# Side jobs of VectorE and GpSimd dealt anew over the slots of a fused attention and FP4 feed-forward kernel

## The chip, the cores and the metric

One NeuronCore of a Trainium2 chip runs the whole kernel in one launch. The metric is the time of one execution on the device in microseconds (us), the median of several runs. Differences of up to about 0.3% can't be told from none.

## The reference

For 16 sequences of 512 tokens with 128 features: a layer norm, then x + attention(xn) + ffn(xn).

```python
q  = (xn @ Wqa @ Wqb)              # 16 heads of 8
k, v = (xn @ Wkva @ Wkvb)          # 4 heads of 8, each shared by 4 query heads
q, k = rope(q), rope(k)
w  = softmax(causal(q @ k.T * 8**-0.5))
attention = (w @ v) @ Wout + bout

def fp4(x):                        # blocks of 16 along the last dimension
    scale = max(max|x| / 6, 1e-12)
    return nearest_of(0, .5, 1, 1.5, 2, 3, 4, 6)(|x / scale|) * sign(x) * scale
ffn = fp4(silu(fp4(xn) @ fp4(w_gate).T) * (fp4(xn) @ fp4(w_up).T)) @ fp4(w_down).T    # 352 hidden
```

## The kernel before

The kernel is one software pipeline over the batches (sequences). Each engine runs its own program of iterations T = -3 to 16, and in iteration T it works on several batches at once: batch T+3's statistics and norm, batch T+2's projections and rope, batch T+1's score maxima and the hidden layer's gate and up products, batch T's exponentials, weighted sums and FP4 rounding of h, and batch T-1's output. A job for a batch outside 0 to 15 is left out, so the first iterations hold little. Semaphores alone order the engines; within an engine the order is that of the program.

An iteration has 8 slots, one for each pair of heads. In a slot TensorE computes six tiles of scores for the row maxima (written (slot, tile) below; three PSUM buffers max_ps in turn, each read by one VectorE reduction of 512, 384 or 256 columns), five tiles of scores for the exponentials (two buffers exp_ps, read by ScalarE), the misc jobs of that slot (two buffers misc_ps: 0 and 1), and a half of one group's weighted sums. Tile n of the maxima waits until VectorE has read tile n-3. The misc jobs are given by a table: gate0 and up0 and then the transposes of xn in slot 0; q and then gate1 and up1 in slot 1; mrow1, qrot and kk in slot 2; gate2, up2 and v in slot 3; gate3 and up3 in slot 4; xqT and out0 in slot 5; out1 and mrow0 in slot 6; the three transposes of h (hqT0 to hqT2, L1152) in slot 7. Output rows are onT times Wout plus three chunks (128, 128, 96 rows) of the FFN's last product (L1164, L1166).

Between the reductions (L713) VectorE does its side jobs, each after a given tile:

- slot 0: `scales` for h (L662 to L666: three small steps to h_scale and h_inv), gated(0) (L726), `magnitudes` of x (L673 and L675 on x_mag)
- slot 1: q_cos (L799), hidden_max(0) (L735), gated(1); slot 2: q_sin (L809), hidden_max(1), k_cos and k_sin
- slot 3: invert(T-1, 1) (L744), the four bn_stats (L831) and bn_aggr (L839), gated(2), the copy of v to v_stage
- slot 4: `magnitudes` of h (L673, L675 on h_mag, 1408 columns of bf16) between (4,0) and (4,1), gated(3), hidden_max(2)
- slot 5: the product onT (L755, two inputs in SBUF), hidden_max(3), output(0); slot 6: maximum of x, output(1); slot 7: `scales` for x, invert(T, 0).

GpSimd, in its order: the causal selects of group 3 (L529, four instructions), split_rest (L552, needs ScalarE's split_high, L962), hidden(0) (L561, h = gate_sb * up_half, 352 columns), steps 1 to 3 of x's rounding (L539, L542, L545; step 1 needs both magnitudes), step 0 of h's (L536, h * h_inv, 1408 columns, needs the h scales), hidden(1), the selects of group 0, V from v_stage (L605), the adds and splits of q and k, hidden(2), the selects of group 1, the variance to rstd (L569 to L574; L572 is a power of 128x4 elements), hidden(3), steps 1 and 2 of h (L539 "h+mag", L542), the selects of group 2, step 3 of h (L545), x_bias = x_res + bias (L643), step 0 of x (L650). TensorE's transposes of h wait for L545; hidden(f) waits for gated(f).

ScalarE evicts and exponentiates; in slot 0, after tile 0, it does split_high and the copy to x_mag (L1010), and after tile 1 th and up_half (L932, L945) of gate0 and up0.

SyncE issues all DMAs. At the start it loads constants, waits until all have landed, and only then runs its iterations; in each, the load of x_in for batch T+4 follows the output stores, and scatter_inverses(T, 0), which waits for invert(T, 0), stands ahead of the second half of the loads of K and Q.

## Time and profile before

| what | value |
|---|---|
| runs | 814.58 us median of 3 (814.21 to 816.49) |
| profiled execution | span 812.0 us from its first to its last instruction; the page gives no other time of it, so the 2.6 us up to the median lie around the span |
| TensorE matmul busy | 731.3 us, 90% |
| VectorE, ScalarE, GpSimd busy | 637.4, 545.0, 613.8 us |
| TensorE's granted clock | mean 0.977 of full; 1.00 in every stretch from 91 to 762 us |
| DMA | 76 MB, about a third of the DMA engines' time |

Every time below is in us from the span's start. A busy TensorE is one with a matmul in flight, so small gaps between starts don't show as idle. The steady part runs from 82 to about 754 us: one iteration every 44.8 us. In the timelines below the iteration of interest has its slots 3 to 7 between 232 and 260.5, and the next iteration's slot 0 begins at 260.5.

### The profile page before, as it was taken

The page shows a single profiled execution, that of the slowest core. Times are in us where ns is not written, and L with a number is a line of the kernel's source. Part 1 is how long each engine was busy: PE and PEld are TensorE (multiplying, and loading weights), DVE is VectorE, ACT ScalarE, POOL GpSimd, SP SyncE. Part 2 cuts the span into 40 slices and gives each one's busy share as a digit, 9 for nine tenths or more (in the row PEclk, how much of TensorE's full clock was granted, in tenths as well). Part 3 has the DMA queues.
Part 4 walks back from the last instruction along what each step waited for, and adds up shares of the span by engine and source line. Part 5 has one row for each costly group of instructions (what it writes and reads, how often), then busy time and mean ns, then how long its engine had stood idle before and what let it go on. Part 6 is the DMA issues. An engine that isn't in the chain of part 4 may idle for free.

```text
span 812.0 us, 18601 instructions
## 1 busy us (share of the span) xinstructions
PE 731.3 (90%) x6541; PEld 445.5 (55%) x6541; DVE 637.4 (78%) x1378; ACT 545.0 (67%) x1154; POOL 613.8 (76%) x707
## 2 busy tenths in 40 slices
PE   2366989999999999999999999999999999999782
PEld 1233545666656565656656565656566565656242
DVE  5569888989888888889898888888898888788200
ACT  1212777768777777777787777677777777575850
POOL 5533697878788897978787887979787888748470
PEclk9978899999999999999999999999999999999996
DMA  4423233333343334343333433343333433330211
GB/s 112 121 57 102 56 100 97 94 101 100 98 116 93 92 113 101 118 105 90 96 108 99 117 95 84 114 104 113 90 94 102 113 90 100 93 93 29 57 48 41
DMA packets 84438, 76.06 MB, mean 94 GB/s; under 512 B 27282, under 2 KB 66162, under 8 KB 84346
## 3 DMA queue, kind: packets, MB, share of 16 engines
q1 hardware_dynamic: 84346, 74.87, 33.9%
q8 instruction: 53, 0.87, 0.5%
q14 instruction: 39, 0.32, 0.1%
HBM read 40.73 MB, written 27.53 MB: 84 GB/s over the span
## 4 chain that ended last, share of the span: by engine, by line
PE 65%; DVE 8%; ACT 7%; DMA 6%; POOL 5%; issue 4%; SPq 4%; POOLq 0%; ACTq 0%; DVEq 0%
PE pv_ps L1109 16%; PE exp_ps L1088 12%; PE max_ps L1073 9%; PE misc_ps L1125 7%; PE max_ps L1074 5%; PE misc_ps L1166 5%; DVE neg_max L713 4%; PE misc_ps L1133 3%; ACT P L909 3%; DMA o_sum<-o_scr 2%; PE misc_ps L1164 2%; PE misc_ps L1152 2%; SPq L418 2%; PE misc_ps L1142 2%; DMA o_scr<-oT 1%
## 5 line engine op out<-in xcount | busy, mean ns | idle before, releaser
L713 DVE TENSOR_REDUCE neg_max<-max_ps 128x1 f32<-128x512 f32 (+3 forms) x768 | 430.6, 591 | 82.8 <-PE max_ps L1074 80.4
L909 ACT ACTIVATE P<-exp_ps 128x512 f32<-128x512 f32 x512 | 295.0, 599 | 166.4 <-PE exp_ps L1088 166.1
L1088 PE MATMUL exp_ps<-Q,K 128*128 128x512 bf16 (+3 forms) x1024 | 243.6, 301 | 9.0 <-ACT P L909 6.7
L1073 PE MATMUL max_ps<-K,Q 128*128 128x384 bf16 (+2 forms) x768 | 199.4, 278 | 24.6 <-DVE neg_max L713 13.5
L1074 PE MATMUL max_ps<-Kd,Q 128*128 128x128 bf16 x1024 | 190.9, 221 | 1.8 <-DVE neg_max L713 1.6
L529 POOL TENSOR_SCALAR_AFFINE_SELECT P<-P 128x512 f32<-128x512 f32 x256 | 162.8, 673 | 27.1 <-ACT P L912 27.1
L1109 PE MATMUL pv_ps<-P,V 128*32 128x512 f32 (+3 forms) x2048 | 164.2, 438 | 1.0 <-POOL P L529 0.8
L1073 PEld LDWEIGHTS max_ps<-K,Q 128*128 128x128 bf16 x768 | 75.1, 100 | 103.0 <-DVE neg_max L713 53.1
L1074 PEld LDWEIGHTS max_ps<-Kd,Q 128*128 128x128 bf16 x1024 | 97.9, 99 | 45.7 <-issue 23.0
L561 POOL TENSOR_TENSOR h<-gate_sb,up_half 128x352 f32<-128x352 f32 x64 | 59.8, 935 | 64.4 <-DVE gate_sb L726 64.4
L1088 PEld LDWEIGHTS exp_ps<-Q,K 128*128 128x128 bf16 x1024 | 81.8, 98 | 42.1 <-ACT P L909 20.5
L1109 PEld LDWEIGHTS pv_ps<-P,V 128*32 128x32 f32 x2048 | 53.6, 109 | 79.6 <-issue 68.5
L1125 PE MATMUL misc_ps<-wguT,xqT 128*128 128x352 f32 x256 | 90.1, 475 | 0.2 <-DVE q_cos L799 0.2
L912 ACT ACTIVATE P<-exp_ps 128x512 f32<-128x512 f32 x128 | 78.0, 610 | 15.5 <-PE exp_ps L1088 15.5
L1125 PEld LDWEIGHTS misc_ps<-wguT,xqT 128*128 128x128 f32 x256 | 48.1, 195 | 17.6 <-issue 1.2
L1166 PE MATMUL misc_ps<-wdT,hqT 128*128 128x128 f32 (+1 forms) x384 | 54.6, 279 | 0.0
L539 POOL TENSOR_TENSOR h<-h,h_mag 128x1408 f32<-128x1408 f32 x16 | 51.2, 3200 | 0.0
L1166 PEld LDWEIGHTS misc_ps<-wdT,hqT 128*128 128x128 f32 (+1 forms) x384 | 49.3, 196 | 0.0
L542 POOL TENSOR_TENSOR h<-h,h_mag 128x1408 f32<-128x1408 f32 x16 | 46.8, 2928 | 1.3
L744 DVE RECIPROCAL o_inv<-o_sum 128x32 f32<-128x32 f32 x32 | 11.3, 352 | 45.9 <-DMA o_sum<-o_scr 45.8
L536 POOL TENSOR_TENSOR h<-h,h_inv 128x1408 f32<-128x1408 f32 x16 | 41.5, 2592 | 0.3 <-DVE h_inv L666 0.3
L545 POOL TENSOR_TENSOR h<-h,h_scale 128x1408 f32<-128x1408 f32 x16 | 41.5, 2594 | 0.0
(108 smaller groups left out, 989.7 us busy)
## 6 DMA issues: line engine op xcount, KB each, us to landing
Q<-q_scr SPq DMA_DIRECT2D x64, 224.0 KB
o_scr<-oT SPq DMA_DIRECT2D x32, 256.0 KB, 3.5
q_scr<-q_split SPq DMA_DIRECT2D x16, 384.0 KB, 2.6
Kd<-K SPq DMA_DIRECT2D x64, 96.0 KB
x_in<-x SPq DMA_DIRECT2D x16, 256.0 KB, 4.6
q_scr<-q_split SPq DMA_DIRECT2D x16, 256.0 KB, 2.9
x_res<-x SPq DMA_DIRECT2D x16, 256.0 KB, 5.7
o_raw<-o_scr SPq DMA_DIRECT2D x32, 128.0 KB
```

The source lines that it names most:

```text
L529: nc.gpsimd.affine_select(out=diag, in_=diag, compare_op=ALU.is_ge, fill=0.0, base=0, pattern=[[0, GH], [1, 128]], channel_multiplier=-1). ...
L539: nc.gpsimd.tensor_tensor(t, t, mag[:, :], ALU.add).then_inc(quant, 1)
L561: nc.gpsimd.tensor_tensor(h[T.par(1)][:, f * F:(f + 1) * F], gate_sb[f % 2][:, :], up_half[f % 2][:, :], ALU.mult).then_inc(h_made, 1)
L713: nc.vector.tensor_reduce(neg_max[:, pr // 4, i, heads[0]:heads[0] + len(heads), pr % 4], max_ps[r % 3][:, 0:len(heads) * n].rearrange("p ...
L909: nc.scalar.activation(P[g % 2][:, hh + r % 2, col:col + 512], ps[:, :], ACT.Exp, scale=SCALE).then_inc(exp_done, 1)
L912: nc.scalar.activation(P[g % 2][:, hh:hh + 2, P_COL[2]:P_COL[2] + 256], ps[:, :].rearrange("p (h q) -> p h q", h=2), ACT.Exp, scale=SCALE) ...
L1073: nc.tensor.matmul(ps[:, col:col + d], Qt, Kt[:, half, g, 0:d], start=True, stop=True)
L1074: last = nc.tensor.matmul(ps[:, col + d:col + n], Qt, Kd[:, half, g, d:n], start=True, stop=True)
L1088: last = nc.tensor.matmul(exp_ps[n % 2][:, col:col + width], K[par][:, half, pr // 2, kb * 128:(kb + 1) * 128], Q[par][:, pr, kb * 128:S], ...
L1109: last = nc.tensor.matmul(pv_ps[32 * j:32 * j + 32, kb * 128:S], V[T.par(off)][:, kb, g, :], P[g % 2][:, j, P_COL[kb]:P_COL[kb] + width], ...
L1125: last = nc.tensor.matmul(ps[:, 0:F], xqT[T.par(1)][:, tok[f]], wguT[:, int(job[0] == "u"), :], start=True, stop=True)
L1166: last = nc.tensor.matmul(ps[:, tok[n]], hqT[0:cn, k, tok[c]], wdT[0:cn, k, :], start=False, stop=(k == 2))
```

## The change

- VectorE: `scales` for h of the next iteration's batch T+1 now stands in slot 7 between (7,3) and (7,4), no longer in slot 0; `magnitudes` of x comes after (0,5) instead of before it; the bn_stats are split, two after (1,5) and two after (2,5); the two steps of h's magnitudes are parted, the first after (4,0), the second after (4,4); hidden_max(3) goes from slot 5 to after (6,4); invert(T, 0) to the end of slot 7.
- GpSimd: step 0 of h (L536) is moved ahead of hidden(0) and of x's steps 1 to 3; x_bias and the copies to V are gone.
- ScalarE: split_high goes from after tile 0 to after tile 1 (behind th and up_half), x_mag from tile 0 to tile 2 of slot 0.
- V is written by VectorE in two copies straight from PSUM, into three tiles in turn; v_stage is gone.
- The bias is row 96 of the last chunk of wdT, met by a row of ones in hqT; output adds x_res alone. x_res is loaded one iteration later, at the head of SyncE's iteration.

```diff
+def third(self, off):
+return (self.t0 + off) % 3
...
 k_split = sb("k_split", [128, 3, 128], BF16)
-v_stage = sb("v_stage", [128, NT, KVH * D])
...
 Kd = sb("Kd", [128, 2, KVH, S], BF16)
-V = [sb(f"V{i}", [128, NT, KVH, 32]) for i in range(2)]
+V = [sb(f"V{i}", [128, NT, KVH, 32]) for i in range(3)]
 P = [sb(f"P{i}", [128, GH, P_WIDTH]) for i in range(2)]
...
     for dst, src in (
-        (bout_sb[:, :], bout.partition_broadcast(128)),
+        (wdT[FC[2][1]:FC[2][1] + 1, 2, :], bout.unsqueeze(0)),
         (w_raw[:, 768:768 + F], wdown),
...
     def iteration(T):
-        if T.has(0):
-            T.wait(sp, x_bias_done, 1, 0, 0)
-            sp.dma_start(x_res[:, :, :], x[T.batch(0)].rearrange("(c p) e -> p c e", p=128)).then_inc(x_res_loaded, 16)
+        if T.has(-1):
+            T.prev().misc_wait(sp, misc_read, "out1")
+            sp.dma_start(x_res[:, :, :], x[T.batch(-1)].rearrange("(c p) e -> p c e", p=128)).then_inc(x_res_loaded, 16)
         scatter_sums(T, -1, 1)
...
     nc.gpsimd.memset(half_neg[:, :], -0.5).then_inc(consts_set, 1)
-    for i in range(2):
+    for i in range(3):
         nc.gpsimd.memset(V[i][:, :, :, :], 0.0).then_inc(pool_const, 1)
...
     nc.gpsimd.memset(ident16[:, :], 0.0).then_inc(pool_const, 1)
-    pool.wait_ge(pool_const, 4)
-    for i in range(2):
+    pool.wait_ge(pool_const, 5)
+    for i in range(3):
...
         split_rest(T, 0, 1)
+        if T.has(0):
+            quantize(T, 0, 0, *hs)
         hidden(T, 0)
...
             nc.gpsimd.tensor_tensor(blocks(w_raw[:, :]), blocks(w_raw[:, :]), spread(w_inv[:, :]), ALU.mult).then_inc(w_step, 1)
-        if T.has(0):
-            quantize(T, 0, 0, *hs)
         hidden(T, 1)
...
             causal(T, 0, 0)
-        if T.has(1):
-            T.prev().misc_wait(pool, misc_read, "v")
-            if T.has(-1):
-                T.wait(pool, pv_done, KVH, -1, KVH)
-            for s in range(2):
-                nc.gpsimd.tensor_copy(V[T.par(1)][:, :, s::2, D * s:D * s + D],
-                                      v_stage[:, :, :].rearrange("p c (g d) -> p c g d", g=KVH)[:, :, s::2, :]).then_inc(v_ready, 1)
         if T.has(2):
...
             quantize(T, 0, 3, *hs)
-        if T.has(0):
-            T.wait(pool, x_res_loaded, 16, 0, 16)
-            T.misc_wait(pool, misc_read, "out1")
-            nc.gpsimd.tensor_tensor(x_bias[:, :, :], x_res[:, :, :],
-                                    bout_sb[:, :].unsqueeze(1).to_broadcast([128, NT, E]), ALU.add).then_inc(x_bias_done, 1)
         if T.has(3):
...
+    def powers_of_two(mag, sem_):
+        m = mag.bitcast(U16)
+        nc.vector.tensor_scalar(m, m, 0x7F80, 0x0040, ALU.bitwise_and, ALU.bitwise_or).then_inc(sem_, 1)
+    def at_least_one(mag, sem_):
+        nc.vector.tensor_scalar(mag, mag, 1.5 * 2.0 ** 22, None, ALU.max).then_inc(sem_, 1)
...
-        m = mag.bitcast(U16)
-        nc.vector.tensor_scalar(m, m, 0x7F80, 0x0040, ALU.bitwise_and, ALU.bitwise_or).then_inc(sem_, 1)
+        powers_of_two(mag, sem_)
         eng_wait(sem_, 1)
-        nc.vector.tensor_scalar(mag, mag, 1.5 * 2.0 ** 22, None, ALU.max).then_inc(sem_, 1)
+        at_least_one(mag, sem_)
...
         if n == 0:
-            T.wait(dve, x_bias_done, 1, -1, 1)
+            T.wait(dve, x_res_loaded, 16, -1, 16)
...
         nc.vector.tensor_tensor(y[:, c, :], misc_ps[0][:, 0:2 * E].rearrange("p (c e) -> p c e", c=2),
-                                x_bias[:, c, :], ALU.add).then_inc(misc_read[0], 1)
+                                x_res[:, c, :], ALU.add).then_inc(misc_read[0], 1)
+    def statistics(T, chunks):
+        if not T.has(3):
+            return
+        T.wait(dve, x_loaded, 16, 3, 16)
+        if 0 in chunks:
+            T.wait(dve, mv_done, NT, 2, NT)
+        for c in chunks:
+            nc.vector.bn_stats(bn_raw[:, c, :], x_in[:, c, :]).then_inc(bn_done, 1)
...
         reduces(0, 0, 1)
-        if T.has(0):
-            T.wait(dve, h_quant, 3, -1, 3)
-            T.wait(dve, h_maxed, NT, 0, NT)
-            scales(lambda s, n: T.wait(dve, s, 3, 0, n) if n else None, h_max[:, :], h_scale[:, :], h_inv[:, :], h_scales, 0)
         reduces(0, 2, 3)
         gated(T, 0)
-        reduces(0, 4)
+        reduces(0, 4, 5)
         if T.has(2):
...
             magnitudes(lambda s, n: T.wait(dve, s, 2, 2, n), x_mag[:, :], x_mags)
-        reduces(0, 5)
         first = T.t0 == FIRST_T + 1
...
         reduces(1, 5)
+        statistics(T, (0, 1))
...
         reduces(2, 5)
+        statistics(T, (2, 3))
...
         invert(T, -1, 1)
-        if T.has(3):
-            T.wait(dve, x_loaded, 16, 3, 16)
-            T.wait(dve, var_done, 2, 2, 2)
-            for c in range(NT):
-                nc.vector.bn_stats(bn_raw[:, c, :], x_in[:, c, :]).then_inc(bn_done, 1)
         reduces(3, 2)
...
+            T.wait(dve, var_done, 2, 2, 2)
             for c in range(NT):
...
-            T.wait(dve, v_ready, 2, 1, 2)
-            nc.vector.tensor_copy(v_stage[:, :, :], misc_ps[1][:, 0:128].rearrange("p (c n) -> p c n", c=NT)).then_inc(misc_read[1], 1)
+            if T.has(-1):
+                T.wait(dve, pv_done, KVH, -1, KVH)
+            for odd in range(2):
+                nc.vector.tensor_copy(V[T.third(2)][:, :, odd::2, D * odd:D * odd + D],
+                                      misc_ps[1][:, 0:128].rearrange("p (c g d) -> p c g d", c=NT, g=KVH)[:, :, odd::2, :]
+                                      ).then_inc(v_ready if odd == 0 else misc_read[1], 1)
         reduces(3, 5)
...
             T.wait(dve, h_powers, NT, 0, NT)
-            magnitudes(lambda s, n: T.wait(dve, s, 2, 0, n), h_mag[:, :], h_mags)
+            powers_of_two(h_mag[:, :], h_mags)
         reduces(4, 1, 2)
...
         hidden_max(T, 2)
-        reduces(4, 4, 5)
+        reduces(4, 4)
+        if T.has(0):
+            T.wait(dve, h_mags, 2, 0, 1)
+            at_least_one(h_mag[:, :], h_mags)
+        reduces(4, 5)
...
         normalize(T)
-        reduces(5, 1, 2)
-        hidden_max(T, 3)
-        reduces(5, 3, 4)
+        reduces(5, 1, 2, 3, 4)
         output(T, 0)
...
         output(T, 1)
-        reduces(6, 3)
-        reduces(6, 4, 5)
+        reduces(6, 3, 4)
+        hidden_max(T, 3)
+        reduces(6, 5)
...
         reduces(7, 2)
+        reduces(7, 3)
+        if T.has(1):
+            T.wait(dve, h_quant, 3, 0, 3)
+            T.wait(dve, h_maxed, NT, 1, NT)
+            scales(lambda s, n: T.wait(dve, s, 3, 1, n) if n else None, h_max[:, :], h_scale[:, :], h_inv[:, :], h_scales, 0)
+        reduces(7, 4, 5)
         invert(T, 0, 0)
-        reduces(7, 3, 4, 5)
+    nc.vector.memset(hqT[FC[2][1]:FC[2][1] + 1, 2, :], 1.0).then_inc(ones_row, 1)
     for k in (K[0], K[1], Kd):
...
             nc.scalar.activation(w_mag[:, :], w_raw[:, :], ACT.Copy, scale=2.0 ** 22).then_inc(w_step, 1)
-        if (slot, r) == (0, 0):
+        if (slot, r) == (0, 1):
             split_high(T, 0, 1)
...
             nc.scalar.activation(q_split[:, 1, :], q_rest[:, :], ACT.Copy).then_inc(q_casts, 1)
-        if (slot, r) == (0, 0) and T.has(2):
+        if (slot, r) == (0, 2) and T.has(2):
             T.wait(act, x_scaled, 1, 2, 1)
...
     pe.wait_ge(proj_ready, 1)
-    pe.wait_ge(pool_const, 10)
+    pe.wait_ge(ones_row, 1)
+    pe.wait_ge(pool_const, 13)
...
             if g == 0:
-                T.wait(pe, v_ready, 2, off, 2)
+                T.wait(pe, v_ready, 1, off, 1)
+                T.prev().prev().misc_wait(pe, misc_read, "v")
         else:
...
             for j in range(GH):
-                last = nc.tensor.matmul(pv_ps[32 * j:32 * j + 32, kb * 128:S], V[T.par(off)][:, kb, g, :],
+                last = nc.tensor.matmul(pv_ps[32 * j:32 * j + 32, kb * 128:S], V[T.third(off)][:, kb, g, :],
                                         P[g % 2][:, j, P_COL[kb]:P_COL[kb] + width],
...
                 nc.tensor.matmul(ps[:, tok[n]], onT[:, tok[c]], wout_sb[:, :], start=True, stop=False)
-                for k, (_, cn) in enumerate(FC):
+                for k, cn in enumerate((FC[0][1], FC[1][1], FC[2][1] + 1)):
                     last = nc.tensor.matmul(ps[:, tok[n]], hqT[0:cn, k, tok[c]], wdT[0:cn, k, :], start=False, stop=(k == 2))
```

## Rows read from the trace of the kernel before

**Rows 1.** Stretches: span, busy us (instructions) by engine, granted clock, DMA share, GB/s.
```profile
134.32:179.10 44.78, 43.98 (x409) 27.37 (x409) 38.70 (x87) 33.69 (x73) 37.93 (x43) 1.00 0.35 95
...
628.10:672.90 44.80, 43.99 (x409) 27.42 (x409) 38.70 (x86) 33.71 (x73) 37.93 (x43) 1.00 0.38 100
```

**Rows 2.** Timeline of TensorE, 223.85 to 268.7: start us, us, instruction [idle before, releaser].
```profile
241.71 0.23 PE L1073 MATMUL max_ps<-K,Q 128*128 128x128 bf16 x1 [0.57 <-DVE neg_max L713]
...
256.38 0.63 PE L1152 MATMUL misc_ps<-ident,h 128*128 128x128 f32 x4
...
266.85 1.02 PE L1133 MATMUL misc_ps<-xnT,proj 128*128 128x512 f32 x2
```

**Rows 3.** Timeline of VectorE and GpSimd, slots 4 to 7 of one iteration.
```profile
239.19 1.00 DVE L673 TENSOR_SCALAR h_mag<-h_mag 128x1408 uint16<-128x1408 uint16 x1
...
240.22 0.83 DVE L675 TENSOR_SCALAR h_mag<-h_mag 128x1408 bf16<-128x1408 bf16 x1
...
244.89 0.74 DVE L755 TENSOR_TENSOR onT<-o_raw,o_spread 128x512 f32<-128x512 f32 x1
...
242.66 1.05 POOL L572 TENSOR_TENSOR rstd<-var_eps,half_neg 128x4 f32<-128x4 f32 x1
...
244.15 0.93 POOL L561 TENSOR_TENSOR h<-gate_sb,up_half 128x352 f32<-128x352 f32 x1
...
245.04 3.32 POOL L539 TENSOR_TENSOR h<-h,h_mag 128x1408 f32<-128x1408 f32 x1
...
253.64 2.59 POOL L545 TENSOR_TENSOR h<-h,h_scale 128x1408 f32<-128x1408 f32 x1
```

**Rows 4.** Waits, 180 to 490: us in total, times, longest us.
```profile
PEld misc_ps L1129 <- ACT up_half L945: 2.9, 7, 0.4
```

**Rows 5.** The chain of waits over the start: start us, us, what.
```profile
21.82 0.70 DVE q_sin L809
...
44.21 0.48 PE max_ps L1073
```

**Rows 6.** Timeline of the start, SyncE's queue and VectorE.
```profile
25.35 0.39 SPq L493 DMA_DIRECT2D x_in<-x  x1
...
31.93 0.86 DVE L831 BATCH_NORM_STATS2 bn_raw<-x_in 128x6 f32<-128x128 f32 x4
```

**Rows 7.** The tile x_in, 20 to 33 us: its load's time to landing.
```profile
DMA to landing us min/median/max: 2.9/2.9/2.9
```

**Rows 8.** Timeline of VectorE, GpSimd and ScalarE, slot 0 (the first row: slot 1).
```profile
225.09 2.59 POOL L536 TENSOR_TENSOR h<-h,h_inv 128x1408 f32<-128x1408 f32 x1
...
264.77 0.94 POOL L561 TENSOR_TENSOR h<-gate_sb,up_half 128x352 f32<-128x352 f32 x1 [2.47 <-DVE gate_sb L726]
...
262.39 0.70 DVE L664 RECIPROCAL h_inv<-h_scale 128x88 f32<-128x88 f32 x1
...
265.21 0.65 DVE L673 TENSOR_SCALAR x_mag<-x_mag 128x512 uint16<-128x512 uint16 x1
...
265.89 0.29 DVE L675 TENSOR_SCALAR x_mag<-x_mag 128x512 bf16<-128x512 bf16 x1
...
263.08 0.48 ACT L945 ACTIVATE up_half<-misc_ps 128x352 f32<-128x352 f32 x1
```

**Rows 9.** Timeline of iteration 13, slots 4 and 5.
```profile
692.50 2.86 POOL L539 TENSOR_TENSOR h<-h,h_mag 128x1408 f32<-128x1408 f32 x1
...
693.86 2.05 DVE L755 TENSOR_TENSOR onT<-o_raw,o_spread 128x512 f32<-128x512 f32 x1
...
696.05 0.46 PE L1164 MATMUL misc_ps<-wout_sb,onT 128*128 128x128 f32 x2 [1.18 <-DVE onT L755]
```

**Rows 10.** Groups by line and form, 225 to 490: busy us, mean ns.
```profile
L1166 PE MATMUL misc_ps<-wdT,hqT 128*128 128x128 f32 x96 | 14.6, 275 | 0.0
...
L1166 PE MATMUL misc_ps<-wdT,hqT 96*128 96x128 f32 x48 | 9.3, 274 | 0.0
```

**Rows 11.** Waits of SyncE's queue, 200 to 490.
```profile
SPq L452 <- DMA i_scr<-o_inv: 37.3, 13, 4.4
```

More of the change, by code:

```diff
@@ L151, in build @@
         wout_sb = sb("wout_sb", [E, E])
-        bout_sb = sb("bout_sb", [128, E])
         cosq_sb = sb("cosq_sb", [128, S])
@@ L203, in build @@
         x_res = sb("x_res", [128, NT, E])
-        x_bias = sb("x_bias", [128, NT, E])
         y = sb("y", [128, NT, E])
@@ L237, in build @@
         const_dma = sem("const_dma")
+        ones_row = sem("ones_row")
         factors_in = sem("factors_in")
@@ L280, in build @@
         x_res_loaded = sem("x_res_loaded")
-        x_bias_done = sem("x_bias_done")
         stored = sem("stored")
@@ L666, in scales, with magnitudes @@
                 nc.vector.tensor_scalar(inv, inv, 1.0 - 2.0 ** -22, None, ALU.mult).then_inc(sem_, 1)
-            def magnitudes(eng_wait, mag, sem_):
+            def powers_of_two(mag, sem_):
                 m = mag.bitcast(U16)
                 nc.vector.tensor_scalar(m, m, 0x7F80, 0x0040, ALU.bitwise_and, ALU.bitwise_or).then_inc(sem_, 1)
+            def at_least_one(mag, sem_):
+                nc.vector.tensor_scalar(mag, mag, 1.5 * 2.0 ** 22, None, ALU.max).then_inc(sem_, 1)
+            def magnitudes(eng_wait, mag, sem_):
+                powers_of_two(mag, sem_)
                 eng_wait(sem_, 1)
-                nc.vector.tensor_scalar(mag, mag, 1.5 * 2.0 ** 22, None, ALU.max).then_inc(sem_, 1)
+                at_least_one(mag, sem_)
             def weight_scales():
```

## The prediction, made before the changed kernel was run

> **What bounds the kernel now.** I read the stretches first. In the steady part one iteration takes 44.8 us and TensorE is busy for 44.0 of them [rows 1]: eleven such stretches between 134 and 673, of which the first and the last are shown (a twelfth, around 500, took 1.3 us more). VectorE is busy for 38.7, ScalarE for 33.7 and GpSimd for 37.9, so work taken from those three is worth nothing by its amount, only where TensorE waits for it. So I looked for the waits of TensorE's queue, first in the timeline. Written (slot, tile) for the score maxima, two places lie in what the change touches. Tile (4,4) waits in every iteration for VectorE, with 0.57 us of idle time, some 0.74 us from start to start, because the two steps on h_mag stand between the reductions of (4,0) and (4,1) [rows 2, 3]. The transposes of xn in slot 0 wait for ScalarE's eviction of up0, 0.41 us a time at the weight load (2.9 over 7), of which I count 0.3 for the matmuls [rows 4]. The third thing to see is a near miss: GpSimd's last step on h ends at 253.64 + 2.59 = 256.23, and the transposes of h start at 256.38 [rows 2, 3]. Whatever TensorE gains in slots 4 to 7 it can keep only if GpSimd gets there sooner too.
>
> Then the chain of waits over the start, where nothing is overlapped: q_sin at 21.82 leads through GpSimd, ScalarE and the DMA queue to the first maximum at 44.21 [rows 5]. A delay of q_sin is a delay of everything.
>
> **The change, part by part.** Sums are against the span of 812.0; the runs' median of 814.58 lies 2.6 above it and I carry that over.
>
> *Statistics of x in slots 1 and 2.* In the steady state this moves 4 x 0.2 us of bn_stats out of slot 3 (the four take 0.86, [rows 6]) into gaps in which VectorE waits for TensorE; x_in has long landed. Worth 0. At the start it is otherwise. In iteration -2 VectorE meets the statistics of batch 1 straight after slot 1's work, ahead of q_sin, and must wait for x_in. SyncE issues that load at 25.35, behind the constants' loads [rows 6], and it takes 2.9 us to land [rows 7]: 28.3. In the kernel before the statistics ran at 31.93 and never waited. After: 28.3 plus two bn_stats (0.4) puts q_sin at 28.75 instead of 21.82. Queued behind it on VectorE are k_cos, k_sin and the weights' steps; GpSimd's q_rope, the splits and the writes of q and k wait for it in turn. Nothing on that chain is shortened, so the first maximum moves by **+6.9**. Bounds: 5.5, if the later copies meet less traffic, to 8, if x_in takes 4 us. The new memset of one row of hqT (some 0.5 us on VectorE) and the third V on GpSimd come before this wait and vanish in it.
>
> *The h scales at the end of the iteration before, the first step on h ahead of x's steps on GpSimd.* Before, GpSimd idled 2.47 us in slot 0 until hidden(0) at 264.77, and then did it [rows 8]. After, it does split_rest, then h x h_inv (2.59 us, [rows 8]), then hidden(0). split_rest waits for ScalarE's split_high, which now follows the eviction of up0 (263.08 + 0.48 = 263.56, [rows 8]; some 0.15 us sooner without the two jobs ahead of it). So the first step on h runs from about 263.75 to 266.35. VectorE came to x_mag's first step at 265.21 [rows 8]; after, the reduction of (0,5) (a third of a microsecond) is ahead of it, less the 0.2 or so that slot 0 gains: 265.3. What do such meetings cost? The trace has three. x_mag's first step takes 0.65 us where hidden(0) is running (265.21 to 265.86, hidden(0) ends at 265.71), and its second 0.29 [rows 8]. The product onT takes 0.74 when it starts ahead of GpSimd's h+mag, and 2.05 when it starts 1.36 after it: it ends 0.55 after h+mag does [rows 3, 9]. And h_mag's steps take 1.00 and 0.83 between GpSimd's selects [rows 3]. In each VectorE's step stands still until GpSimd's instruction is over. Carried over: the first step is held from 265.3 to 266.35 and ends at 266.55; hidden(0), waiting by then, goes next, and the second step is held to 267.45 and ends at 267.65. VectorE pays 2.3 us where it paid 0.9. Queued behind are the reduction of (1,0) and q_cos: (1,0) is read at 267.65 + 0.7 = 268.35, while TensorE wants to overwrite it with (1,3), which follows the q product, at 266.85 + 1.24 [rows 2] less the 0.15 gained so far: 267.95. That is 0.4. And up1 needs the bank that q_cos reads out 0.2 us late. I take **+0.6** an iteration, for the 14 iterations from 0 to 13 that have both steps: **+8.4**. Bounds: 0, if the third PSUM buffer swallows it, and 1.4, the whole hold. I choose near the middle, since the q product (1.02 us, [rows 2]) gives VectorE some time back.
>
> The Trainium skill says the same as a rule (SBUF — State Buffer, Who interferes with whom): VectorE and GpSimd share a pair of ports under an exclusive lock, and the second to issue is blocked for the other's whole instruction. The trace agrees: 2.05 against 0.74 [rows 3, 9].
>
> *h_mag's two steps apart, hidden_max(3) to slot 6.* The reduction of (4,1) starts when the first step ends, at 240.12, instead of the second, at 240.98 [rows 3], and (4,4) waits no more: 0.74 us for TensorE at this place. What is late next is GpSimd's last step on h. Its run from the selects of slot 4 to 256.23 has no gap, and none of it is removed; x_bias is behind it. It gains only the 0.28 that one select loses to h_mag's second step. That step now stands behind four reductions and two small steps, some 3.0 us after 240.12: at 243.1, on GpSimd's power of the variance (1.05 us for four elements, 242.66 today and 0.28 sooner then, so until 243.4, [rows 3]). If it is not held, TensorE's transposes of h start 0.28 sooner; if it is, the two delays cancel and onT and h+mag keep their places: 0. I take **-0.14** x 12 = **-1.7**; bounds 0 and -0.28, and -0.74 an iteration if GpSimd's run shrinks in a way I don't see.
> By the lock rule of the Trainium skill (SBUF — State Buffer, Who interferes with whom) even that tiny power blocks VectorE for all of its time. By it this term would be 0 and the sum 1.7 higher; no row here has such a pair, so I do not lean on it.
>
> *ScalarE's split_high and x_mag behind th and up0.* up0 is read in time and the wait of 0.3 in slot 0 goes [rows 4]. Against it, the three steps of the h scales (0.70 for the reciprocal alone, 1.13 in all, [rows 8]) now stand in slot 7 ahead of (7,4), and two of them meet GpSimd's xq and selects; the second maximum of the next slot 0 needs (7,4) read and comes about 0.15 late. Net **-0.15** x 14 = **-2.1**; bounds -0.4 and +0.2.
>
> *Bias as row 96 of the last weight chunk; V from PSUM; invert last.* A matmul over 96 rows takes 274 ns and one over 128 takes 275 [rows 10], so 97 rows cost nothing. GpSimd loses x_bias and the V copies, both where it isn't awaited: 0; uncovered they'd be worth their 1.7 us an iteration. VectorE writes V in two copies for one, in slot 3, which got lighter: 0, and 0.2 uncovered. invert(T,0) moves back by 1.6 us, and SyncE's queue with it; but SyncE waited 2.9 us a time, and up to 4.4, for the write of the inverses to land (37.3 over 13, [rows 11]) while x_in's load ran, and later it waits less: 0, upper bound +0.5 an iteration if the loads of K and Q push into the scatter of oT.
>
> Sum: 6.9 + 8.4 - 1.7 - 2.1 = 11.5, on the span 823.5, on the median **826.0**.
>
> **The rivals.** The measurement tells about 0.3% (2.4 us) from no change.
> *A, the forecast (0.54):* start and slot 1 both pay. Own range 819 to 832.
> *B, only the start pays (0.22):* the hold of x_mag is swallowed by the PSUM buffers, or the step comes before GpSimd's. Then 6.9 - 1.7 - 2.1 = +3.1, 817.7; with the gains at their bounds (-0.28 x 12 and -0.4 x 14) 812.6. For it speaks that TensorE is seldom more than half a microsecond ahead of VectorE.
> *C, faster (0.17):* at (4,4) the whole 0.74 and in slot 0 the whole 0.3 are kept, and x_mag costs nothing: -1.04 x 14 = -14.6, with the start -7.7, 806.9. It decides at the transposes of h: GpSimd's run must end 0.74 earlier. Break-even is a steady gain of 0.5 an iteration. Against it stands the gapless run [rows 3].
> *D, onT loses its race (0.07):* onT starts 0.15 us ahead of h+mag today [rows 3]. If it comes behind, it is held for up to 2.86 us, as in iteration 13, where TensorE lost 1.18 [rows 9]. At +1.5 an iteration for 12 iterations 18 us come on top: 844. My walk has onT waiting during hidden(3), ahead of h+mag by 0.3, so it should win.
>
> **Numbers.** Faster: C and the lowest end of B, 0.20. Same (812.1 to 817.0): almost half of B, and what C and A have there, 0.18. Slower: 0.62. Range 812 to 832: it leaves out C (most of it), D and A's tail, about 2 in 10.
>
> **What would show it.** Right: VectorE's q_sin of iteration -2 near 28.7 behind a wait for x_in, the first maximum near 51; x_mag's first step at about 1.2 us and the second at 1.1, GpSimd's first step on h beside them; a period of 45.1 to 45.3; no wait at (4,4), but one for GpSimd at the transposes of h. Wrong: a first maximum before 49.5; x_mag's steps under 0.7; a period under 44.5, with GpSimd's last step on h 0.5 us earlier after slot 3; or onT at 2 us and more in every iteration.

## The result, and the profile of the changed kernel

The changed kernel takes **821.53 us** (median; 818.39 to 823.31 over 7 executions) against 814.58 for the kernel before it: a ratio of 1.0083, 95% interval 1.0061 to 1.0106. It is slower, by 7.0 us, where 11.5 were forecast. A second measurement, on the chip that ran the second group of experiments, gave 823.47 against 815.26, 1.0103 (1.0090 to 1.0117). The profiled execution took 823.3 with a span of 821.3, against a span of 812.0 before: 9.3 more, part of it the scatter of single executions.

The start first: the timeline of the changed kernel from 24 to 29 us, and its first maximum.

```profile
24.93 0.39 SPq L493 DMA_DIRECT2D x_in<-x  x1
27.75 0.49 DVE L770 BATCH_NORM_STATS2 bn_raw<-x_in 128x6 f32<-128x128 f32 x2 [7.48 <-DMA x_in<-x]
28.16 0.67 DVE L807 TENSOR_TENSOR q_sin<-misc_ps,sinq_sb 128x512 f32<-128x512 f32 x1
...
50.57 0.48 PE L1084 MATMUL max_ps<-K,Q 128*128 128x384 bf16 x1 [9.15 <-DMA Kd<-K]
```

VectorE stands for 7.48 us in front of the statistics until x_in lands, q_sin comes at 28.16 instead of 21.82, and the first maximum at 50.57 instead of 44.21 [rows 5, 6]: +6.36.

The stretches of the steady part, from q_cos to q_cos (columns as in [rows 1]):

```profile
185.10:229.93 44.83, 43.91 (x405) 27.44 (x410) 39.55 (x87) 34.17 (x73) 36.08 (x41) 1.00 0.38 103
634.06:678.97 44.91, 43.95 (x405) 27.44 (x410) 40.05 (x88) 34.16 (x73) 36.30 (x41) 1.00 0.36 98
```

The period went from 44.77 to 44.90 (the first of these has a slot 5 that is 0.07 shorter). GpSimd is busy for 1.6 to 1.9 us less in it [rows 1] and VectorE for 0.9 to 1.4 more, part of which is standing still inside an instruction. Slots 0 and 1 show it, in the timeline of VectorE, GpSimd and TensorE that answers to [rows 8].

```profile
270.04 2.59 POOL L536 TENSOR_TENSOR h<-h,h_inv 128x1408 f32<-128x1408 f32 x1
...
271.63 1.14 DVE L658 TENSOR_SCALAR x_mag<-x_mag 128x512 uint16<-128x512 uint16 x1
272.59 0.98 POOL L561 TENSOR_TENSOR h<-gate_sb,up_half 128x352 f32<-128x352 f32 x1
...
272.81 0.91 DVE L662 TENSOR_SCALAR x_mag<-x_mag 128x512 bf16<-128x512 bf16 x1
...
274.84 0.67 DVE L796 TENSOR_TENSOR q_cos<-misc_ps,cosq_sb 128x512 f32<-128x512 f32 x1
...
275.56 0.30 PEld L1137 LDWEIGHTS misc_ps<-wguT,xqT 128*128 128x128 f32 x2 [0.55 <-DVE q_cos L796]
```

x_mag's first step ends at 272.77, just behind GpSimd's h x h_inv (272.63), and its second at 273.72, just behind hidden(0) (273.57). Together 2.05 us where it was 0.94. The last line shows who pays: up1's weight load waits for q_cos.

Slots 4 to 7, the lines that answer to [rows 3]:

```profile
248.78 1.27 POOL L572 TENSOR_TENSOR rstd<-var_eps,half_neg 128x4 f32<-128x4 f32 x1
249.51 0.51 DVE L662 TENSOR_SCALAR h_mag<-h_mag 128x1408 bf16<-128x1408 bf16 x1
250.49 0.93 POOL L561 TENSOR_TENSOR h<-gate_sb,up_half 128x352 f32<-128x352 f32 x1
250.87 1.10 DVE L748 TENSOR_TENSOR onT<-o_raw,o_spread 128x512 f32<-128x512 f32 x1
251.38 3.31 POOL L539 TENSOR_TENSOR h<-h,h_mag 128x1408 f32<-128x1408 f32 x1
...
266.01 0.68 DVE L653 TENSOR_SCALAR h_inv<-h_inv 128x88 f32<-128x88 f32 x1
```

And iteration 13, the lines that answer to [rows 9]:

```profile
699.13 2.85 POOL L539 TENSOR_TENSOR h<-h,h_mag 128x1408 f32<-128x1408 f32 x1 [0.92 <-DVE h_mag L662]
699.91 2.62 DVE L748 TENSOR_TENSOR onT<-o_raw,o_spread 128x512 f32<-128x512 f32 x1
...
702.68 0.46 PE L1176 MATMUL misc_ps<-wout_sb,onT 128*128 128x128 f32 x2 [1.87 <-DVE onT L748]
...
704.22 1.49 PE L1178 MATMUL misc_ps<-wdT,hqT 128*128 128x128 f32 x6
```

To see where a period gains and loses, I took the start of the first product with V in each slot (the timeline of TensorE, line 1121 of the changed kernel) and subtracted neighbours. Two of its rows, the products of slots 0 and 1 of one iteration:

```profile
225.92 1.28 PE L1121 MATMUL pv_ps<-P,V 128*32 128x512 f32 x16
232.00 1.28 PE L1121 MATMUL pv_ps<-P,V 128*32 128x384 f32 x16
```

Slot 1's length is 232.00 - 225.92 = 6.08; each column is the stretch that ends where its own slot's product starts. Nearly all these lengths agree to 0.02 us from iteration to iteration, so they can be set side by side (medians; two values where iterations alternate; slots 2, 3 and 6 are 5.56, 5.79 and 5.72 in every kernel).

| kernel | slot 0 | slot 1 | slot 4 | slot 5 | slot 7 | period |
|---|---|---|---|---|---|---|
| before | 5.48 | 5.61 | 5.46 | 6.10 | 5.04 | 44.77 |
| changed | 5.37 | 6.08 | 4.95 | 6.32 | 5.11 | 44.90 |
| a1_start | 5.37/5.14 | 6.08 | 4.95 | 6.33 | 5.12 | 44.92/44.70 |
| a2_h0, a3_both | 5.37/5.14 | 5.61 | 4.95 | 6.33 | 5.12 | 44.45/44.22 |
| b1_stats | 5.48 | 5.61 | 5.46 | 6.10 | 5.04 | 44.76 |
| b2_mag | 5.48 | 5.61 | 4.95 | 6.33 | 5.26 | 44.70 |
| b3_bias_v | 5.48 | 5.61 | 5.46 | 6.10 | 4.91 | 44.63 |
| b4_mag_bias_v | 5.48 | 5.61 | 4.95 | 6.33 | 5.12 | 44.57 |
| a5_race | 5.37 | 5.61 | 4.95 | 6.19 | 4.99 | 44.17 |
| a6_scale3 | 5.14 | 5.61 | 4.95 | 6.32 | 5.11 | 44.19 |
| a7_act | 5.48 | 5.61 | 4.95 | 6.33 | 5.12 | 44.56 |
| c1_best | 5.14 | 5.61 | 4.95 | 6.19 | 4.99 | 43.94 |

Three steps that were costed from [rows 4, 10, 11] have their answers here: the group of the last weight chunk, 225 to 490 us, at 274 ns with 97 rows as with 96, and the waits of SyncE's queue, 200 to 490, which fell from 37.3 to 24.4. The wait of xn's transposes for up0 is no longer in the view of the waits.

```profile
L1178 PE MATMUL misc_ps<-wdT,hqT 97*128 97x128 f32 x48 | 9.3, 274 | 0.0
```
```profile
SPq L452 <- DMA i_scr<-o_inv: 24.4, 13, 2.6
```

### The profile page after: what moved, and what is told of

It reads as the page before. It is cut to its first block, busy times and chain, and to the rows that moved or that the text cites. A ratio compares the mean times of both kernels' runs of the same rounds, so it can differ in the third digit from the quotient of the medians.

```text
span 821.3 us, 18452 instructions
## 1 busy us (share of the span) xinstructions
PE 729.2 (89%) x6450; PEld 447.1 (54%) x6541; DVE 654.6 (80%) x1395; ACT 550.6 (67%) x1154; POOL 587.5 (72%) x662
## 4 chain that ended last, share of the span: by engine, by line
PE 56%; DVE 17%; ACT 7%; DMA 5%; issue 5%; SPq 5%; POOL 4%; another core or an unknown queue 1%; ACTq 0%; POOLq 0%; DVEq 0%
PE pv_ps L1121 13%; DVE neg_max L706 9%; PE exp_ps L1099 9%; PE max_ps L1084 8%; PE misc_ps L1137 8%; PE misc_ps L1178 5%; PE max_ps L1085 4%; ACT P L919 4%; PE misc_ps L1145 3%; PE misc_ps L1176 2%; PE misc_ps L1154 2%; PE misc_ps L1170 1%; DVE q_sin L807 1%; POOL P L529 1%; DVE h_inv L651 1%
## 5 line engine op out<-in xcount | busy, mean ns | idle before, releaser
L1099 PE MATMUL exp_ps<-Q,K 128*128 128x128 bf16 (+3 forms) x933 | 209.6, 293 | 11.7 <-ACT P L919 6.8
L529 POOL TENSOR_SCALAR_AFFINE_SELECT P<-P 128x512 f32<-128x512 f32 x256 | 158.1, 653 | 38.7 <-ACT P L922 38.7
L1085 PEld LDWEIGHTS max_ps<-Kd,Q 128*128 128x128 bf16 x1024 | 100.3, 99 | 43.5 <-issue 23.3
L1137 PE MATMUL misc_ps<-wguT,xqT 128*128 128x352 f32 x256 | 93.6, 480 | 0.2 <-DVE q_cos L796 0.2
L1178 PE MATMUL misc_ps<-wdT,hqT 128*128 128x128 f32 (+1 forms) x384 | 55.5, 282 | 0.0
L1178 PEld LDWEIGHTS misc_ps<-wdT,hqT 128*128 128x128 f32 (+1 forms) x384 | 50.0, 198 | 0.0
L637 POOL TENSOR_TENSOR xq<-xn,x_inv 128x512 f32<-128x512 f32 x16 | 16.9, 1058 | 36.6 <-DVE x_inv L653 35.9
L1176 PE MATMUL misc_ps<-wout_sb,onT 128*128 128x128 f32 x128 | 26.8, 291 | 16.6 <-DVE onT L748 15.6
```

The source lines that it names most:

```text
L529: nc.gpsimd.affine_select(out=diag, in_=diag, compare_op=ALU.is_ge, fill=0.0, base=0, pattern=[[0, GH], [1, 128]], channel_multiplier=-1). ...
L1085: last = nc.tensor.matmul(ps[:, col + d:col + n], Qt, Kd[:, half, g, d:n], start=True, stop=True)
L1099: last = nc.tensor.matmul(exp_ps[n % 2][:, col:col + width], K[par][:, half, pr // 2, kb * 128:(kb + 1) * 128], Q[par][:, pr, kb * 128:S], ...
L1137: last = nc.tensor.matmul(ps[:, 0:F], xqT[T.par(1)][:, tok[f]], wguT[:, int(job[0] == "u"), :], start=True, stop=True)
L1178: last = nc.tensor.matmul(ps[:, tok[n]], hqT[0:cn, k, tok[c]], wdT[0:cn, k, :], start=False, stop=(k == 2))
```

## The experiments

"a" kernels start from the changed kernel, "b" kernels from the one before. Each group of four shared a chip and its runs of the kernel before.

**First group: the two costs (kernel before: 814.0).** In a1_start the statistics of iteration -2 alone go back to slot 3; in a2_h0 GpSimd's first step on h goes back; a3_both has both; b1_stats puts the statistics forward in the kernel before.

```
a1:              reduces(1, 5)
-                statistics(T, (0, 1))
+                early = T.t0 != FIRST_T + 1
+                if early:
+                    statistics(T, (0, 1))
...
                 invert(T, -1, 1)
+                if not early:
+                    statistics(T, range(NT))
a2:              split_rest(T, 0, 1)
-                if T.has(0):
-                    quantize(T, 0, 0, *hs)
                 hidden(T, 0)
...
+                if T.has(0):
+                    quantize(T, 0, 0, *hs)
                 hidden(T, 1)
```

a1_start. 

> The changed kernel with one thing left as before, in iteration -2 alone: the four statistics of batch 1 stand in slot 3 again, not ahead of q_sin. If the wait for x_in at the start costs what the traces show at the first maximum (50.57 against 44.21), q_sin of iteration -2 is back near 22 us, the first maximum near 44.2, and the time falls by 6.4, from 821.5 to about 815. The rival: the start's delay is swallowed later, because the first iterations wait for something else (TensorE's clock, the loads of K and Q); then the time falls by less than 3.

Measured: 816.86, ratio 1.0029 (1.0014 to 1.0043), the first maximum at 45.24. By the ratios that is 4.4 to 6.0 us less than the changed kernel's two measurements; the rival (under 3) falls. Of the start 1.0 is left (45.24 against 44.21), and the forecast had let it vanish in the wait. 0.65 of it is there at q_sin (22.47 against 21.82) and is the memset of the bias' row: 0.48 us at the head of VectorE's memsets, and b3_bias_v, which has it too, has q_sin at 22.46. The memset of the third V tile stands on GpSimd, which waits 4.06 us for VectorE behind it. The rest comes after q_sin and is partly scatter: in the eight kernels with this start the first maximum comes between 44.70 and 45.27.

a2_h0. 

> The changed kernel with GpSimd's first step on h (h times the inverse scale) behind the steps on x again, as before. If holding x_mag's two steps behind it is what lengthens slots 0 and 1 (x_mag's first step 1.14 and second 0.91 us against 0.65 and 0.29; slots 0 to 1 are 0.3 to 0.47 us longer a time), the steps go back under 0.7 and 0.4, the period falls from 44.90 to about 44.45, and the time falls by 0.47 x 14 = 6.6 to about 815. The rival: the hold is paid by nobody, and the longer slots come from q_cos and up1 through TensorE's own order; then the steps shorten and the time stays at 821 within 2.

Measured: 816.83, ratio 1.0026 (1.0011 to 1.0041). The two steps in its timeline, where only hidden(0) is beside them, as in the kernel before:

```profile
267.87 0.94 POOL L561 TENSOR_TENSOR h<-gate_sb,up_half 128x352 f32<-128x352 f32 x1 [0.78 <-DVE gate_sb L719]
268.64 0.32 DVE L658 TENSOR_SCALAR x_mag<-x_mag 128x512 uint16<-128x512 uint16 x1
268.99 0.29 DVE L662 TENSOR_SCALAR x_mag<-x_mag 128x512 bf16<-128x512 bf16 x1
...
271.06 0.69 DVE L796 TENSOR_TENSOR q_cos<-misc_ps,cosq_sb 128x512 f32<-128x512 f32 x1 [0.29 <-PE misc_ps L1145]
```

The steps take 0.61 instead of 2.05 and q_cos waits for TensorE, not the other way round. Slot 1 is back at 5.61, and it is the only slot that moved apart from slot 0, which a6_scale3 explains. The rival falls. By the ratios the time is 4.6 to 6.3 less than the changed kernel's.

a3_both. 

> The changed kernel with both put back: the statistics of iteration -2 in slot 3, and GpSimd's first step on h behind the steps on x. If the two costs are separate they add up: 821.5 - 6.4 - 6.6 = about 808.5, under the kernel before, and the gain of the parted steps on h_mag shows. If they overlap or the gain of slot 4 is given back at the transposes of h, it is 812 to 815.

Measured: 810.06, ratio 0.9940 (0.9922 to 0.9957). The two costs are separate: with both gone the rest of the change is a gain of 0.6%.

b1_stats. 

> The kernel before with one part of the change alone: the statistics of x in slots 1 and 2 in every iteration. If they cost only the start, q_sin of iteration -2 comes near 28 us behind a wait for x_in, the first maximum near 50.5, the period stays 44.77, and the time is 814.6 + 6.4 = 821. The rival: statistics in slots 1 and 2 also cost or give in the steady state (the period differs from 44.77 by more than 0.05).

Measured: 820.32, ratio 1.0063 (1.0041 to 1.0084), that is 5.1 us, with 3.3 to 6.8 as its interval. From the timeline of b1_stats and its stretches:

```profile
25.21 0.39 SPq L493 DMA_DIRECT2D x_in<-x  x1
28.02 0.49 DVE L777 BATCH_NORM_STATS2 bn_raw<-x_in 128x6 f32<-128x128 f32 x2 [8.37 <-DMA x_in<-x]
...
50.32 0.48 PE L1081 MATMUL max_ps<-K,Q 128*128 128x384 bf16 x1 [8.62 <-DMA Kd<-K]
```
```profile
184.37:229.12 44.75, 43.94 (x410) 27.41 (x408) 38.71 (x85) 33.69 (x72) 37.85 (x44) 1.00 0.38 103
```

The first maximum moved by 6.11, and no slot of the steady part by more than 0.01: in the steady state the move is worth nothing.

**Second group: slots 4, 5, 0 and the race (kernel before: 815.26).**

after_again. 

> The changed kernel again, unaltered, so that the others of this group can be set against it on the same chip: 820.5 to 822 us; the period 44.90, with the third step of the h scales at 0.68 us and slot 0 at 5.37 us in nearly every iteration.

Measured: 823.47, as told above, with the period at 44.90; the reference for this group.

a5_race, the order of a3_both with one exchange on VectorE (`normalize` is the product onT):

```
                 reduces(4, 4)
+                normalize(T)
                 if T.has(0):
                     T.wait(dve, h_mags, 2, 0, 1)
...
                 reduces(5, 0)
-                normalize(T)
                 reduces(5, 1, 2, 3, 4)
```

> The changed kernel with both costs put back (as in a3_both, 810.1 us), and VectorE's order altered at one more place: the product onT ahead of h_mag's second step, where it can't come behind GpSimd's h+mag. If slot 5 is 0.23 us longer than before because the first out0 waits for onT, and iterations 13 and 14 lose 2.8 us because onT comes behind h+mag, then slot 5 goes back to about 6.10, onT takes 1.1 us or less in iterations 13 and 14 too, and the time falls by 0.2 x 12 + 2.8 = about 5, to 805. The rival: GpSimd's run is the limit of slots 5 to 7, its h+mag starts later behind the later second step, and the transposes of h wait for it what slot 5 gains; then only the 1.5 to 2.8 us of the last iterations come, 807 to 808.5.

Measured: 807.37, ratio 0.9907 (0.9892 to 0.9924). Against a3_both's ratio that is 0.33% or 2.7 us. In its timeline, iteration 3 and then iteration 15, the last that quantizes h:

```profile
241.19 1.05 POOL L572 TENSOR_TENSOR rstd<-var_eps,half_neg 128x4 f32<-128x4 f32 x1
241.91 0.67 DVE L748 TENSOR_TENSOR onT<-o_raw,o_spread 128x512 f32<-128x512 f32 x1
242.51 0.52 DVE L662 TENSOR_SCALAR h_mag<-h_mag 128x1408 bf16<-128x1408 bf16 x1
243.98 2.86 POOL L539 TENSOR_TENSOR h<-h,h_mag 128x1408 f32<-128x1408 f32 x1
...
764.14 0.69 DVE L748 TENSOR_TENSOR onT<-o_raw,o_spread 128x512 f32<-128x512 f32 x1 [5.30 <-issue]
764.75 0.52 DVE L662 TENSOR_SCALAR h_mag<-h_mag 128x1408 bf16<-128x1408 bf16 x1
...
765.35 2.87 POOL L539 TENSOR_TENSOR h<-h,h_mag 128x1408 f32<-128x1408 f32 x1 [3.95 <-DVE h_mag L662]
```

The steady part gained 0.27 a period (0.14 in slot 5, 0.13 in slot 7): onT takes 0.67 instead of 1.10 and, what counts more, h+mag takes 2.86 instead of 3.31, so the whole run of GpSimd on h is over sooner. In iteration 13 slot 5 fell from 7.86 to 6.19. But in iteration 15 h_mag's step now stands behind an onT that waits for its inverses, and GpSimd idles 3.95 us before h+mag. TensorE then waits 1.95 us for GpSimd's last step on h, and a wait for it is not there in a3_both. From the last q_cos to the end a5_race takes 142.0 us and a3_both 141.7, so at the end nothing is left of what the race gave. The steady gain of 0.27 a period (3.2 in 12) is larger than the 0.2 expected; iteration 15 was missed. So the time came out where the rival had it (807 to 808.5), but not for its reason: h+mag starts 0.19 later, as it said, and is over 0.26 sooner.

a6_scale3: `reduces(7, 4, 5)` becomes `reduces(7, 4)`, the third step of the h scales, `reduces(7, 5)`.

> As a3_both (810.1 us), with the third step of the h scales behind the reduction of (7,4) instead of ahead of it. In a3_both slot 0 takes 5.37 us where that step takes 0.68 (held behind GpSimd's select) and 5.14 where it takes 0.21. If this hold is what makes slot 0 longer, slot 0 takes 5.14 in every iteration, the period is 44.22, and the time falls by 0.23 x 10 = 2.3, to 807.8. The rival: slot 0's two lengths have another cause that the step only follows; then both lengths stay and the time is 810 within 0.5.

Measured: 807.36, ratio 0.9906 (0.9893 to 0.9919). Slot 0 is at 5.14 in every iteration. The pair that led to it stands in a3_both's own timeline, two iterations that are otherwise alike:

```profile
523.55 0.21 DVE L653 TENSOR_SCALAR h_inv<-h_inv 128x88 f32<-128x88 f32 x1
...
523.55 2.47 POOL L529 TENSOR_SCALAR_AFFINE_SELECT P<-P 128x512 f32<-128x512 f32 x4 [0.83 <-ACT P L927]
...
612.24 0.68 DVE L653 TENSOR_SCALAR h_inv<-h_inv 128x88 f32<-128x88 f32 x1
...
612.22 2.40 POOL L529 TENSOR_SCALAR_AFFINE_SELECT P<-P 128x512 f32<-128x512 f32 x4 [0.82 <-ACT P L927]
```

In the first the two have the same start and the step takes 0.21; in the second the select is 0.02 us ahead, the step takes 0.68, and slot 0 is 0.23 longer. (The starts alone don't tell who is first: at 434.87 in the same trace they are equal too, and the step takes 0.69.) In the changed kernel the select is ahead (265.99 against 266.01), and the step takes 0.67 to 0.69 in all eleven iterations from 221 to 671 us.

b2_mag parts h_mag's steps and moves the last h maximum in the kernel before (the diff's lines on `powers_of_two`, `at_least_one` and `hidden_max(T, 3)`, nothing else).

> The kernel before with one part of the change alone: h_mag's two steps parted, and the last h maximum in slot 6. By the forecast's step GpSimd's gapless run lets TensorE keep only 0.14 us an iteration: 814.0 - 1.7 = 812.3. By the traces of the changed kernel slot 4 gives 0.51, slot 5 takes 0.23 and slot 7 0.05: a period of 44.5, minus 2.7 in the steady part, of which the last two iterations take back up to 2.8 because onT comes behind h+mag: 811 to 814. If the gain of the changed kernel needed the lighter GpSimd (no x_bias, no copies of V), the transposes of h wait here for 0.3 us or more an iteration and the period is above 44.65.

Measured: 814.24, ratio 0.9992 (0.9977 to 1.0007): no difference. Slot 4 gives 0.51, slot 5 takes 0.23 and slot 7 takes 0.22, so 0.07 a period is left. GpSimd's last step on h ends 32.96 us after the q_cos of its iteration, 33.03 before: its run got 0.07 shorter and that is what TensorE kept. The forecast's step holds (0.14, bounds 0 and 0.28), and better than my later reading of a period of 44.5. The period of 44.70 lies above the 44.65 that was to mean that the lighter GpSimd has a part in the changed kernel's gain; the third group finds it.

**Third group: ScalarE's order, bias and V, and the best version (kernel before: 814.53).**

a7_act is a6_scale3 with `split_high` and the x_mag copy at (0, 0) again.

> As a6_scale3 (807.4 us, slot 0 at 5.14 us), with ScalarE's split_high and x_mag copy ahead of th and up0 again, as before. If the wait of the transposes of xn for up0's eviction was worth its 0.3 to 0.4 us to TensorE, slot 0 goes back to 5.45 to 5.5, the period is 44.5, and the time rises by 0.33 x 13 = 4.3, to 811.7. The rival: the wait at the weight load is hidden behind the matmuls; slot 0 stays within 0.05 of 5.14 and the time at 807.4.

Measured: 813.06, ratio 0.9975 (0.9955 to 0.9995), 5.6 us over a6_scale3 by the ratios. The wait is back in the view of the waits, 225 to 490:

```profile
PEld misc_ps L1152 <- ACT up_half L966: 2.5, 6, 0.4
```

Slot 0 takes 5.48 instead of 5.14. ScalarE's order was worth 0.34 a period; the rival falls.

b3_bias_v and b4_mag_bias_v have the bias row, V from PSUM, the load of x_res one iteration later and no x_bias, in the order of the kernel before and in that of b2_mag.

> The kernel before with the bias row and V from PSUM alone (three V tiles, no x_bias and no copies of V on GpSimd, x_res loaded ahead), everything else in its old order. The forecast costed this at nothing: period 44.77, time within 1 us of the kernel before. The rival: GpSimd's lighter run lets the transposes of h start sooner, or VectorE's second copy of V costs slot 3 up to 0.2 us; then the period moves by 0.1 or more and the time by 1.3 or more.

> b2_mag (h_mag's steps parted, period 44.70, slot 7 at 5.26 us) and the bias row and V from PSUM together. In the changed kernel slot 7 takes 5.12. If the 0.14 us come from the lighter GpSimd, slot 7 is at 5.12 here, the period at 44.56, and the time 0.14 x 12 = 1.7 under b2_mag's. The rival: they come from the h scales or ScalarE's order, and slot 7 stays at 5.26.

Measured: b3 813.56, ratio 0.9987 (0.9967 to 1.0008); b4 814.54, ratio 0.9995 (0.9976 to 1.0014). In time neither can be told from no change, and b4 not from b2_mag. In the traces slot 7 is 0.13 shorter with the bias row in one pair and 0.14 in the other. The cause is not where I had looked, at GpSimd's run on h (it ends 32.96 and 32.97 us after q_cos with and without x_bias). It is in the timeline of b2_mag, and then that of b4_mag_bias_v:

```profile
255.66 0.64 DVE L662 TENSOR_SCALAR x_scale<-x_max 128x32 f32<-128x32 f32 x1
...
254.99 1.27 POOL L643 TENSOR_TENSOR x_bias<-x_res,bout_sb 128x512 f32<-128x512 f32 x1
```
```profile
256.38 0.17 DVE L649 TENSOR_SCALAR x_scale<-x_max 128x32 f32<-128x32 f32 x1
```

With x_bias beside it the first step of x's scales is held until x_bias ends (256.26) and takes 0.64; without it, 0.17. It stands ahead of the reduction of (7,2). In the kernel before, the same pair costs the step less, and there too slot 7 has 0.13 to give:

```profile
257.07 0.43 DVE L662 TENSOR_SCALAR x_scale<-x_max 128x32 f32<-128x32 f32 x1
...
256.19 1.27 POOL L643 TENSOR_TENSOR x_bias<-x_res,bout_sb 128x512 f32<-128x512 f32 x1
```

That this hold is the whole of the 0.13 and 0.14 is read from the place and not shown: no run leaves out x_bias alone, and the copies of V go with it.

c1_best joins a5_race and a6_scale3.

> Both reorderings together: the statistics of iteration -2 and GpSimd's first step on h put back (as in a3_both), onT ahead of h_mag's second step (as in a5_race) and the third step of the h scales behind the reduction of (7,4) (as in a6_scale3). Their gains lie in different slots: slots 5 and 7 at 6.19 and 4.99 us, slot 0 at 5.14. If they add, the period is 43.95 and the time 807.4 - 0.23 x 12 = 804.6. The rival: GpSimd's run or TensorE's own work (some 44.0 us busy in a period) sets a floor just under 44.2, and the time stays at 806 to 807.5.

Measured: **803.78**, ratio 0.9855 (0.9825 to 0.9885), 1.45% under the kernel before. The gains add, slot by slot. Its stretch:

```profile
222.56:266.50 43.94, 43.79 (x410) 27.56 (x408) 37.97 (x86) 33.77 (x72) 35.99 (x41) 1.00 0.38 103
```

TensorE is busy for 43.79 of 43.94 us, so it hardly ever stands idle here. That is no proof of a floor: small gaps between starts don't show as idle, and the busy time itself was 43.98 before. What stays in iteration 15 (GpSimd's 3.87 us of idle time before h+mag) might be had by keeping the old order there; that wasn't run.

## Why the prediction came out as it did

The sign and the two main mechanisms (the start and slot 1) were right; the size was 11.5 where 7.0 and 8.2 were measured. By its steps, with what the runs showed:

| step | forecast | shown |
|---|---|---|
| statistics of iteration -2 wait for x_in | +6.9 once | +6.1 at the first maximum in b1_stats, +6.4 with V and the memset |
| h x h_inv ahead of x's steps, slot 1 | +0.6 a period | +0.47 (a2_h0) |
| h_mag's steps apart | -0.14 | -0.07 (b2_mag) |
| ScalarE's order, slot 0 | -0.3 | -0.34 (a7_act) |
| h scales in slot 7, slot 0 | +0.15 | +0.23 (a6_scale3) |
| bias row, V from PSUM | 0 | -0.14 (b3, b4) |
| sum of a period | +0.31 | +0.15; the period itself +0.13 |

*The start.* The load landed 2.8 us after its issue, as read, but it was issued 0.42 earlier than in the trace of before (24.93 against 25.35), and that is most of the difference; that VectorE's and GpSimd's added memsets cost nothing because the wait covers them holds for this kernel (+6.36) and no longer for a1_start.

*x_mag.* The walk was right to a tenth: first step 1.14 and second 0.91 where "about 1.2" and "1.1" were named, and the queue of VectorE gave TensorE back all but 0.47. The term was 0.13 x 14 = 1.8 us too large, and its two places were weighed the wrong way round. At tile (1,3), put at 0.4, TensorE loses 0.21 (0.59 from the start of (1,2) to that of (1,3), at 273.78 and 274.37, against 0.38 in a2_h0); up1's wait for q_cos, put at 0.2, has the other 0.26. Rival B, in which the buffers swallow it, is out.

*h_mag.* "TensorE can keep only what GpSimd gains" is what b2_mag shows. Rival C, which kept all of it, is out. What was not seen is the place: I had the gain given back at the transposes of h, but half of it is lost earlier, in slot 5, where onT meets hidden(3), takes 1.10 instead of 0.74 and ends at 251.97, and the first out0 starts 0.15 after it. With onT ahead (a5_race) 0.14 of the 0.23 come back. What sets the sum, though, is GpSimd's run. From the timeline of the kernel before, and then that of b2_mag:

```profile
238.58 2.97 POOL L529 TENSOR_SCALAR_AFFINE_SELECT P<-P 128x512 f32<-128x512 f32 x4
```
```profile
237.46 2.68 POOL L529 TENSOR_SCALAR_AFFINE_SELECT P<-P 128x512 f32<-128x512 f32 x4
...
241.25 1.27 POOL L572 TENSOR_TENSOR rstd<-var_eps,half_neg 128x4 f32<-128x4 f32 x1
```

The selects give the 0.29 that the forecast counted. h_mag's second step was to be held by the power or not; instead it isn't held and the power takes 1.27 where it took 1.05 [rows 3], so 0.07 is left, and that is the period's gain. In a5_race the power takes 1.05 and h+mag 2.86, GpSimd's last step on h ends 0.26 sooner after q_cos than in a3_both, and the period gains 0.27.

*The term costed at nothing that wasn't.* x_bias lay where nobody waits for it, so it was priced at 0, though the trace of before had x's first scale step beside it at 0.43 us. A meeting was looked for only where VectorE's work was moved, not where GpSimd's was taken away. Worth 0.14 x 12 = 1.7 us.

*Rival D* happened, but only where I had not placed it. In the steady iterations onT stays ahead of h+mag, as walked. In iterations 13 and 14, where x's work is gone and GpSimd reaches h+mag early, onT comes behind and takes 2.62; TensorE waits 1.87 and slot 5 of iteration 13 takes 9.37 us against 7.20. Only 0.66 of these 2.17 are the longer wait. In after_again, the same kernel, TensorE waits 1.89 there and slot 5 takes 7.86; its granted clock stays at 1.00 where that of the first execution is at 0.58 (last section):

```profile
703.00:706.00 3.00, 3.00 (x36) 2.48 (x39) 2.10 (x6) 0.60 (x1) 2.40 (x2) 1.00 0.42 104
```

In iteration 14 it is the other way round: 7.74 and 9.37, against 7.19 before. From the last q_cos (iteration 13) to the end the changed kernel's two executions take 142.3 and 141.2 us and the one before 139.8. The last product with V parts this stretch; here it is in the changed kernel and then in the kernel before:

```profile
798.28 2.37 PE L1121 MATMUL pv_ps<-P,V 128*32 128x512 f32 x32 [0.81 <-POOL P L529]
```
```profile
788.84 2.37 PE L1109 MATMUL pv_ps<-P,V 128*32 128x512 f32 x32 [0.81 <-POOL P L529]
```

Up to it the changed kernel takes 119.3 us and the one before 116.7. The other traces fall in line: with the old order 117.0 (b1_stats) and 116.7 (b3_bias_v); with h_mag's steps parted and onT behind them, nine traces with this one, 118.2 (after_again) to 120.5 (a1_start); with onT ahead, 117.1 (a5_race). So the race costs 1.2 us at the least, where waits alone are counted (0.66 and 0.55), and more where the clock falls after them. Behind the product most take 22.8 to 23.4; b1_stats, with the old order, takes 24.7, because its last matmuls keep the lower clock (1.49 us for six to the end, elsewhere 0.83), so the total alone would mislead.

The spans' difference of 9.3 adds up: 6.76 by the q_cos of iteration 1 (140.42 against 133.66); 0.04 in the twelve periods to iteration 13 (678.97 against 672.17), where about 1.3 of the changed kernel's longer period stand against the 1.3 that the execution of before lost once around 500; and 2.5 at the end. For the median, a start of 6.4 and 12 x 0.13 = 1.6 make 8.0, against 7.0 and 8.2 measured. The forecast had 6.9 and 4.6. The end, with its 1.4 and 2.5 in the two traces, would come on top, and it was forecast at nothing; how much of it the medians hold is open.

The errors partly cancelled. The forecast was too high by x_mag (1.8), by x_bias, put at nothing (1.7), and by the start (0.5). It was too low by h_mag, whose gain it put at 1.7 where 0.07 x 12 = 0.8 was had, by ScalarE's order with the h scales (a gain of 2.1 forecast, of 0.11 x 14 = 1.5 shown), and by the end. That the sum was no further off is in part luck.

Of the signs that were named, q_sin (28.16), the first maximum (50.57), x_mag's steps (1.14 and 0.91) and the missing wait at (4,4) are there. The period, at 44.90, is below the 45.1 to 45.3 named. A wait of TensorE for GpSimd at the transposes of h is not in the view of the waits; they start 0.14 us behind GpSimd's last step on h (262.56 and 262.70).

## What to carry to other kernels

When an instruction moves on one of two engines that hold each other up, list every instruction of the other that it will meet at the new place, and every one that it leaves free at the old place: here such meetings, of both signs and 0.1 to 0.5 us an iteration, made up the steady part of the result together with ScalarE's order. A gain at one wait should be followed to the next thing that is late before it is counted; here 0.51 us became 0.07. And order changes that are free in the steady part must be read once more at the two ends, where loads have not landed and neighbours are missing: there they cost 6.4 us at the start, and at the end they took back what the race's repair had given.
